# Moving twelve low-part subtractions from VectorE to GpSimd and all raw dot products into the first counting window, in a GAT + RGCN kernel

## The chip, the cores and the metric

One core of a Trainium2 chip runs the program. The metric is the device time of one execution in microseconds; the profile's span leaves out a small part at its ends. All times here are in microseconds (us) unless marked ns.

## The reference

A two-layer graph network on 625 nodes with 1024 features and 20000 edges (sorted by destination):

```python
h = x @ W
al, ar = h @ a_l, h @ a_r
e = exp(-leaky_relu(al[src] + ar[dst], 0.1))
rowsum = segment_sum(e, src)
h_prime = segment_sum(e[:, None] * h[dst], src) / (rowsum[:, None] + EPS)
x = layernorm(x + elu(h_prime))
# second layer: x @ root + bias + sum over 8 relations of mean-aggregated x @ weight[r], a gate, tanh, layernorm
```

## The kernel before, in words

**Precision.** Every fp32 matrix is split into a high part (a cast to fp32r) and a low part (`raw - high`, by a tensor_tensor subtraction); a product is three matmuls: high by high, low by high, high by low. So each operand costs one cast (ScalarE) and one subtraction (VectorE or GpSimd). The result is collected in PSUM.

**First product, h = xT by W.** W comes in two column halves of eight chunks (128x512) each, through a ring of four buffers (`w_raw`, `w_hi`, `w_lo`). SyncE loads a chunk when the low part four chunks earlier is made (line 337); ScalarE casts it when TensorE has used the buffer (line 527); VectorE makes `w_lo` (`split_low`, line 800). `w_lo_done` counts the low parts, for all chunks in order. h's first half (five tiles of 128 rows) is drained by ScalarE, a cast to `h_part(0, 0, t)` and a copy to `h_raw` (`copy_h`, line 551). `h_raw` shares memory with parts of the second half of h.

**Counting edges.** Edges are turned into a matrix of counts per destination, relation and source by one-hot matmuls, in 40 windows of 16 destinations. `oh_s` (one-hots of the sources, made in eight pieces at line 808 from two f16 tiles in SBUF) is the stationary side. For each pass over five edge tiles VectorE writes five `hot` buffers (line 931, a tensor_scalar of the f16 `table`, with a column of `key`), TensorE multiplies them (line 1281). A window has one pass or more. The five buffers are handed back and forth by the semaphores `built` and `counted`, so VectorE can be at most one pass ahead. ScalarE copies the window's counts out (line 568).

**What is woven into the windows.** After the passes of window w, each engine does other work, fixed by window numbers: TensorE the remaining items of W's second half in windows 0 to 6 (`items`, line 300; two or three items of three matmuls each), later the sums and transposes of counts and the attention's products (`att_h`, line 1253, from `hp_w(j)` on: windows 23, 25 and 33 for the first three tiles). VectorE: in window 0 the low parts of W's chunks 5 to 7 (`split_low(1, AHEAD + n)`), the five low parts of h's first half (`low_h`, line 875) and seven of ten dot products of h with a (`dot_raw`, line 888; `scalar_tensor_tensor` of `h_raw` and `a_bc`, both in SBUF, each waiting for the one before), the other three in windows 1 to 3; in windows 7 to 13 it drains h's second half; then, per destination tile j, `leaky`, `att_mult` (line 910; windows 20, 22, 30, 38 and after the last) and `att_low` (line 916; windows 22, 24, 32, 39 and after the last). ScalarE does `add_ar`, `exp_e` and `att_high` (the cast before `att_low`, in the window of `att_mult`). `tmp` has two buffers, so `add_ar(j)` waits for `att_low(j - 2)`.

**GpSimd** writes six iotas at the start and then waits until all 40 windows are counted (line 476); from then on it makes the low parts of all later weights (line 460). The last low parts of the kernel (line 465) run beside VectorE's `u - xf` (line 1104), two SBUF tiles of 128x1024.

The lines 1054, 1057 and 1059, named in the rows, belong to the second layer: a reduction of `C_hi`, a cast of `col_sum` (one SBUF tile of 128x640) and a subtraction of two SBUF tiles of 128x640.

Of the kernel before, what the change touches and what calls it, by code (L numbers as in the profile page):

```python
# [5 lines left out]
def gat_rgcn_kernel(nc, dst_cols, src_cols, type_cols, dst_units, xT, x, weights, a, bias, b_gate, counts_dram, out):  # L6
    f32 = mybir.dt.float32
# [5 lines left out]
    ALU = mybir.AluOpType  # L13
# [6 lines left out]
    KT = D // P  # L20
    NT = -(-N // P)
# [15 lines left out]
    WINDOWS = NP // WIN  # L37
# [14 lines left out]
    def rows(t):  # L52
        return P if t < NT - 1 else N - P * (NT - 1)
# [5 lines left out]
    with ctx:  # L59
# [6 lines left out]
        M_hi = [sb("M_hi0", [P, KT, NP], f32r)]  # L66
# [41 lines left out]
        def h_part(low, half, t, p=P):  # L108
            return h_parts[0:p, 2 * half + low, t, :]
# [58 lines left out]
        def bank(b, p=P, c0=0, c=H2):  # L168
            return ps[0:p, b * H2 + c0:b * H2 + c0 + c]
# [4 lines left out]
        def xw_bank(t):  # L174
            return t if t < NT - 1 else 7
# [118 lines left out]
        ALL = KT * NT  # L294
        AHEAD = 5
        SPREAD = 7
        DOTS_AHEAD = 7
        WARM = 8

        def items(w):  # L300
# [143 lines left out]
        @block.gpsimd  # L444
        def _(pool):
            pool.iota(iota_i[:, :], pattern=[[1, CODES], [P // 2, WIN]], base=0, channel_multiplier=0).then_inc(pool_consts, 1)
            pool.iota(part_col[:, :], pattern=[[0, 1]], base=0, channel_multiplier=1,
                      allow_small_or_imprecise_dtypes=True).then_inc(pool_consts, 1)
            pool.iota(iota_s[:, :], pattern=[[1, P]], base=0, channel_multiplier=0,
                      allow_small_or_imprecise_dtypes=True).then_inc(pool_consts, 1)  # L450
            pool.iota(iota_up[:, :, :], pattern=[[1, SUB], [SUB, UNITS]], base=1, channel_multiplier=0,
                      allow_small_or_imprecise_dtypes=True).then_inc(pool_consts, 1)
            pool.iota(iota_down[:, :, :], pattern=[[-1, SUB], [-SUB, UNITS]], base=1000, channel_multiplier=0,
                      allow_small_or_imprecise_dtypes=True).then_inc(pool_consts, 1)
            pool.iota(iota_body[:, :], pattern=[[BODY, ALL_TILES // BODY]], base=0, channel_multiplier=0,
                      allow_small_or_imprecise_dtypes=True).then_inc(pool_consts, 1)

            def split_chunk(n, k):
                pool.wait_ge(w_hi_done, 8 * n + k + 1)
                pool.tensor_tensor(w_lo[k % RING][:, :], w_raw[k % RING][:, :], w_hi[k % RING][:, :].bitcast(f32),  # L460
                                   ALU.subtract).then_inc(w_lo_done, 1)

            def last_chunk(k):
                pool.wait_ge(last_hi_done, k + 1)
                pool.tensor_tensor(last_w(1, k), last_raw[k][:, :], last_w(0, k).bitcast(f32),
                                   ALU.subtract).then_inc(last_lo_done, 1)

            def split_ahead(n, last=False):
                for k in range(KT):
                    if k < KT - RING:  # L470
                        split_chunk(n, k + RING)
                    elif not last:
                        split_chunk(n + 1, k + RING - KT)


            pool.wait_ge(window_counted, WINDOWS)
            for k in range(RING):
                split_chunk(SEG_Z, k)

            def x1_low(t):  # L480
                pool.wait_ge(x1_hi_done, t + 1)
                pool.tensor_tensor(x1_lo[0:rows(t), t, :], u[0:rows(t), t, :], x1_hi[0:rows(t), t, :].bitcast(f32),
                                   ALU.subtract).then_inc(x1_lo_done, 1)

            split_chunk(SEG_Z, RING)
            split_chunk(SEG_Z, RING + 1)
            x1_low(0)
            split_chunk(SEG_Z, RING + 2)
            x1_low(1)
            split_chunk(SEG_Z, RING + 3)  # L490
            x1_low(2)
            split_chunk(SEG_Z + 1, 0)
            x1_low(3)
            split_chunk(SEG_Z + 1, 1)
            x1_low(4)
            split_chunk(SEG_Z + 1, 2)
            split_chunk(SEG_Z + 1, 3)
            split_ahead(SEG_Z + 1)
            with pool.Fori(0, R // 2) as j:
                for half in range(4):  # L500
                    split_ahead(4 * j + SEG_U + half)
            split_ahead(SEG_U + 2 * R)
            pool.wait_ge(g_drained, ITEMS + ITEMS * R)
            for k in range(KT):
                split_chunk(SEG_U + 2 * R + 1 + (k + RING) // KT, (k + RING) % KT)
                if k < NT:
                    r = slice(0, rows(k))
                    pool.tensor_tensor(xf[r, k, :], x1_hi[r, k, :].bitcast(f32), x1_lo[r, k, :].bitcast(f32), ALU.add)\
                        .then_inc(xf_done, 1)
            split_chunk(SEG_G, RING)  # L510
            for k in range(3):
                last_chunk(k)
            split_chunk(SEG_G, RING + 1)
            for k in range(3, 5):
                last_chunk(k)
            split_chunk(SEG_G, RING + 2)
            for k in range(5, 7):
                last_chunk(k)
            split_chunk(SEG_G, RING + 3)
            last_chunk(7)  # L520
# [3 lines left out]
        def _(act):  # L524
# [25 lines left out]

            def copy_h(half, t):
                act.wait_ge(u_ready, NT * half + t + 1)
                nc.scalar.copy(h_part(0, half, t, rows(t)), bank(xw_bank(t), rows(t))).then_inc(h_hi_done, 1)
                if half == 0:
                    nc.scalar.copy(h_raw[0:rows(t), t, :], bank(xw_bank(t), rows(t))).then_inc(u_drained, 1)
# [216 lines left out]
        def _(dve):  # L772
# [27 lines left out]
            def split_low(n, k):  # L800
                dve.wait_ge(w_hi_done, 8 * n + k + 1)
                v.tensor_tensor(w_lo[k % RING][:, :], w_raw[k % RING][:, :], w_hi[k % RING][:, :].bitcast(f32),
                                ALU.subtract).then_inc(w_lo_done, 1)
# [68 lines left out]
            v.tensor_copy(lohi_row[:, :], ps[0:1, 6 * H2:6 * H2 + WINDOWS]).then_inc(row_done, 1)  # L872
            dve.wait_ge(row_done, 1)

            def low_h(t):
                r = slice(0, rows(t))
                dve.wait_ge(h_hi_done, t + 1)
                dve.wait_ge(u_drained, NT + t + 1)
                v.tensor_tensor(h_part(1, 0, t, rows(t)), h_raw[r, t, :], h_part(0, 0, t, rows(t)).bitcast(f32),
                                ALU.subtract).then_inc(h_lo_done, 1)  # L880

            def dot(half, lr, t, source, junk):
                r = slice(0, rows(t))
                at = (2 * half + lr) * NT + t
# [51 lines left out]
            for w in range(WINDOWS):  # L936
                first_pass = window_range(DVE_ENGINE, w)
                dve.reg_mod(tile_at, first_pass, STARTS)
                with dve.Fori(first_pass, LOOP_END, STARTS + BODY):
                    hots(w)  # L940
                if w == 0:
                    split_low(1, AHEAD)
                    for t in range(NT):
                        low_h(t)
                    split_low(1, AHEAD + 1)
                    dve.wait_ge(a_here, 16)
                    for n in range(DOTS_AHEAD):
                        dot_raw(n)
                    split_low(1, AHEAD + 2)
                elif w <= 2 * NT - DOTS_AHEAD:  # L950
                    dot_raw(DOTS_AHEAD + w - 1)
                if SPREAD <= w < AL_W:
                    a, b = [len(DRAINS) * n // (AL_W - SPREAD) for n in (w - SPREAD, w - SPREAD + 1)]
                    for t, piece in DRAINS[a:b]:
                        drain_h(t, piece)
                if w == AL_W:
                    dve.wait_ge(dot_done, 4 * NT)
                    step(v.tensor_tensor(alr[:, :], dots[:, 0:2 * NT], dots[:, 2 * NT:4 * NT], ALU.add))
                    for t in range(NT):
                        d = v.tensor_scalar(diag[:, t * P:(t + 1) * P], ident, alr[:, t:t + 1], None, ALU.mult)  # L960
                    d.then_inc(diag_done, 1)
                for j in range(NT):
                    if w == E_W[j] + 2:
                        leaky(j)
                for j in range(NT - 1):
                    if w == MULT_W[j]:
                        att_mult(j)
                for j in range(NT - 1):
                    if w == min(MULT_W[j] + 2, WINDOWS - 1):
                        att_low(j)  # L970

            att_mult(NT - 1)
            att_low(NT - 1)
            dve.wait_ge(sums_ready, 1)
            v.tensor_scalar(rowsum[:, :], bank(SUM_BANK, c=2 * NT).rearrange("p (t c) -> p t c", c=2)[:, :, 0],
# [554 lines left out]
```

## Time and profile before

| | us |
|---|---|
| median of 3 runs | 1001.15 |
| lowest, highest | 1000.7, 1001.23 |
| the profiled execution, device time | 1000.9 |
| its span | 998.8 |
| TensorE busy (share of the span) | 981.4 (98%) |
| VectorE busy | 391.7 (39%) |
| ScalarE busy | 281.1 (28%) |
| GpSimd busy | 255.0 (26%) |

The granted TensorE clock is full in all 40 slices of the span. Matmuls are pipelined and their recorded durations overlap, so their starts are to be read, not their lengths. In a timeline row the first number is the start from the span's start, the second the time until the last of the grouped instructions ended, x5 the number of them, and in brackets the idle time of the engine before it and what ended it. In the rows PE is TensorE, DVE VectorE, ACT ScalarE, POOL GpSimd.

### The profile page before, as it was taken

Reading aid. Unit: us, or ns where it says so; the run is one execution under the profiler, and the core shown is the slowest. Engines: PE = TensorE matmul, PEld = TensorE weight load, DVE = VectorE, ACT = ScalarE, POOL = GpSimd, SP = SyncE. Lnnn points to the kernel's source line nnn. Section 1 sums busy time; section 2 is a strip of 40 time slices with the busy share of each in tenths; the row PEclk is TensorE's granted clock in tenths of the full one; section 3 lists DMA queues with packets and bytes.
Section 4 is the critical chain, followed back from the end, with each engine's and each line's share of the span. In section 5 each row is a group of like instructions: output and inputs, shape, how many; then the busy total and the mean of one; then the engine's idle time right before and its main releaser. Section 6 shows DMA issues by size and latency. Waiting matters only on the chain.

```text
span 998.8 us, 14624 instructions
## 1 busy us (share of the span) xinstructions
PE 981.4 (98%) x5159; PEld 823.9 (82%) x5159; DVE 391.7 (39%) x746; ACT 281.1 (28%) x487; POOL 255.0 (26%) x196
## 2 busy tenths in 40 slices
PE   9997999999999999999999999999999999999997
PEld 7875677788888888888888888888888888888886
DVE  7979773721431430530430341232232233202277
ACT  4324542851122221221222222222212212212332
POOL 0000002055423223123122142142232232326730
PEclk9999999999999999999999999999999999999999
DMA  7303558066211411311321231141041041212402
GB/s 264 95 12 106 163 154 252 1 214 189 92 36 43 142 52 42 134 57 42 114 78 42 98 94 42 47 134 42 14 168 42 21 161 41 74 46 72 137 1 103
DMA packets 69005, 91.41 MB, mean 92 GB/s; under 512 B 9396, under 2 KB 35475, under 8 KB 68838
## 3 DMA queue, kind: packets, MB, share of 16 engines
q1 hardware_dynamic: 68966, 90.90, 29.0%
q8 instruction: 23, 0.38, 0.2%
q14 instruction: 16, 0.13, 0.0%
HBM read 75.19 MB, written 15.69 MB: 91 GB/s over the span
## 4 chain that ended last, share of the span: by engine, by line
PE 98%; DVE 1%; issue 1%; ACT 0%; POOL 0%; DVEq 0%; ACTq 0%
PE ps L1175 21%; PE ps L1177 21%; PE ps L1176 21%; PE ps L1431 9%; PE ps L1430 9%; PE ps L1281 6%; PE ps L1243 1%; PE ps L1256 1%; PE ps L1257 1%; PE ps L1258 1%; PE ps L1486 1%; PE ps L1485 1%; PE ps L1484 1%; PE ps L1264 1%; PE ps L1328 0%
## 5 line engine op out<-in xcount | busy, mean ns | idle before, releaser
L460 POOL TENSOR_TENSOR w_lo<-w_raw,w_hi 128x512 fp32r<-128x512 f32 x168 | 218.1, 1303 | 701.8 <-ACT w_hi L535 545.7
L535 ACT CAST w_hi<-w_raw 128x512 fp32r<-128x512 f32 x184 | 114.7, 623 | 466.0 <-PE ps L1177 396.0
L1175 PE MATMUL ps<-w_hi,M_hi 128*128 128x512 f32 (+1 forms) x550 | 215.6, 392 | 0.1
L1177 PE MATMUL ps<-w_lo,M_hi 128*128 128x512 f32 (+1 forms) x550 | 214.3, 390 | 0.0
L1176 PE MATMUL ps<-w_hi,M_lo 128*128 128x512 f32 (+1 forms) x550 | 214.2, 389 | 0.0
L1049 DVE SCALAR_TENSOR_TENSOR u<-ps,scale,u 128x512 f32<-128x512 f32 (+1 forms) x90 | 66.4, 744 | 314.2 <-PE ps L1177 314.2
L1430 PE MATMUL ps<-C_hi,x_hi 128*128 128x320 f32 (+3 forms) x640 | 184.4, 306 | 0.0
L1431 PE MATMUL ps<-C_hi,x_lo 128*128 128x320 f32 (+3 forms) x640 | 184.3, 306 | 0.0
L1175 PE MATMUL ps<-w_hi,M 128*128 128x512 f32 (+1 forms) x360 | 140.3, 390 | 0.0
L1177 PE MATMUL ps<-w_lo,M 128*128 128x512 f32 (+1 forms) x360 | 140.2, 390 | 0.0
L1176 PE MATMUL ps<-w_hi,M 128*128 128x512 f32 (+1 forms) x360 | 140.2, 389 | 0.0
L1430 PEld LDWEIGHTS ps<-C_hi,x_hi 128*128 128x128 f32 (+1 forms) x640 | 120.7, 189 | 0.9
L1175 PEld LDWEIGHTS ps<-w_hi,M_hi 128*128 128x128 f32 (+1 forms) x550 | 101.9, 185 | 23.5 <-issue 0.6
L1431 PEld LDWEIGHTS ps<-C_hi,x_lo 128*128 128x128 f32 (+1 forms) x640 | 120.9, 189 | 0.3
L1177 PEld LDWEIGHTS ps<-w_lo,M_hi 128*128 128x128 f32 (+1 forms) x550 | 101.8, 185 | 23.0
L1176 PEld LDWEIGHTS ps<-w_hi,M_lo 128*128 128x128 f32 (+1 forms) x550 | 101.9, 185 | 22.3
L1177 PEld LDWEIGHTS ps<-w_lo,M 128*128 128x128 f32 (+1 forms) x360 | 66.7, 185 | 15.0
L1176 PEld LDWEIGHTS ps<-w_hi,M 128*128 128x128 f32 (+1 forms) x360 | 66.7, 185 | 14.8
L1175 PEld LDWEIGHTS ps<-w_hi,M 128*128 128x128 f32 (+1 forms) x360 | 66.7, 185 | 14.5
L931 DVE TENSOR_SCALAR hot<-table,key 128x640 bf16<-128x640 f16 x210 | 65.7, 381 | 21.3 <-PE ps L1281 19.1
L1281 PE MATMUL ps<-hot,oh_s 128*128 128x320 bf16 x420 | 64.0, 299 | 3.2 <-DVE hot L931 1.3
L1054 DVE TENSOR_REDUCE col_sum<-C_hi 128x640 f32<-128x3200 f32 x8 | 47.9, 5992 | 43.5 <-DMA C_hi<-C_dram 43.5
(178 smaller groups left out, 771.9 us busy)
## 6 DMA issues: line engine op xcount, KB each, us to landing
w_raw<-weights SPq DMA_DIRECT2D x184, 256.0 KB, 2.8
C_dram<-Cst SPq DMA_DIRECT2D x25, 512.0 KB, 6.0
C_hi<-C_dram SPq DMA_DIRECT2D x8, 1600.0 KB, 7.0
z<-b_gate SPq DMA_DIRECT2D x5, 512.0 KB, 9.9
u<-bias SPq DMA_DIRECT2D x5, 512.0 KB, 7.6
xT_raw<-xT SPq DMA_DIRECT2D x8, 312.5 KB, 6.0
u<-x SPq DMA_DIRECT2D x4, 512.0 KB, 5.2
last_raw<-weights SPq DMA_DIRECT2D x8, 256.0 KB, 6.0
```

The source lines that it names most:

```text
L460: pool.tensor_tensor(w_lo[k % RING][:, :], w_raw[k % RING][:, :], w_hi[k % RING][:, :].bitcast(f32), ALU.subtract).then_inc(w_lo_done, 1)
L535: nc.scalar.copy(w_hi[k % RING][:, :], w_raw[k % RING][:, :]).then_inc(w_hi_done, 1)
L931: v.tensor_scalar(hot[:, s * NP:(s + 1) * NP], table[:, :], float(WIN * w), key[:, ds(tile + s, 1)], ALU.add, ALU.is_equal).then_inc(built ...
L1049: v.scalar_tensor_tensor(u[r, t, half * H2:(half + 1) * H2], bank(t, rows(t)), scale[odd][r, t:t + 1], u[r, t, half * H2:(half + 1) * H2], ...
L1054: v.tensor_reduce(col_sum[:, :], C_hi[:, :, :].bitcast(f32).rearrange("p m n -> p n m"), X, ALU.add)\
L1175: mm(o, lhs_hi[:, k, c], w_hi[k % RING][:, :], start=opens, stop=False)
L1176: mm(o, lhs_lo[:, k, c], w_hi[k % RING][:, :], start=False, stop=False)
L1177: last = mm(o, lhs_hi[:, k, c], w_lo[k % RING][:, :], start=False, stop=closes_)
L1243: last = mm(o, ident_r[:, :], Cst[j % 2][:, m0:m1, r, :], start=r == 0, stop=r == R - 1)
L1281: last = mm(bank(window_bank(w) + c, c=SPLIT), oh_s[:, ds(edge + s * P, P)], hot[:, s * NP + c * SPLIT:s * NP + (c + 1) * SPLIT], start=Fa ...
L1430: mm(o, x1_hi[r, m, f], C_hi[r, m, c0:c0 + cn], start=m == 0, stop=False)
L1431: last = mm(o, x1_lo[r, m, f], C_hi[r, m, c0:c0 + cn], start=False, stop=m == NT - 1)
```

## The change

GpSimd's program gets a part ahead of its wait for the last window: the five low parts of h's first half, then (when VectorE has made the first five low parts of W's second half, so that the count stays in order) those of chunks 5 to 7, then `att_low` for tiles 0 to 3. VectorE loses these and does all ten `dot_raw` in window 0, after the hots. ScalarE's copy of h's second half now waits for all five low parts of h; VectorE waits for the four low parts of the attention before its own last one, to keep the count in order. The hunks of the diff are, from the top, in GpSimd's, ScalarE's and VectorE's program; VectorE's own definition of `low_h` goes too.

```diff
+            def low_h(t):
+                pool.wait_ge(h_hi_done, t + 1)
+                pool.wait_ge(u_drained, NT + t + 1)
+                pool.tensor_tensor(h_part(1, 0, t, rows(t)), h_raw[0:rows(t), t, :], h_part(0, 0, t, rows(t)).bitcast(f32),
+                                   ALU.subtract).then_inc(h_lo_done, 1)
+
+            def att_low(j):
+                pool.wait_ge(attT_hi_done, j + 1)
+                pool.tensor_tensor(M_lo[0][:, j, :], tmp[j % 2][:, :], M_hi[0][:, j, :].bitcast(f32), ALU.subtract)\
+                    .then_inc(attT_lo_done, 1)
+
+            for t in range(NT):
+                low_h(t)
+            pool.wait_ge(w_lo_done, KT + AHEAD)
+            for k in range(AHEAD, KT):
+                split_chunk(1, k)
+            for j in range(NT - 1):
+                att_low(j)
 
             pool.wait_ge(window_counted, WINDOWS)
...
             def copy_h(half, t):
                 act.wait_ge(u_ready, NT * half + t + 1)
+                if half == 1:
+                    act.wait_ge(h_lo_done, NT)
...
                 if w == 0:
-                    split_low(1, AHEAD)
-                    for t in range(NT):
-                        low_h(t)
-                    split_low(1, AHEAD + 1)
                     dve.wait_ge(a_here, 16)
-                    for n in range(DOTS_AHEAD):
+                    for n in range(2 * NT):
                         dot_raw(n)
-                    split_low(1, AHEAD + 2)
-                elif w <= 2 * NT - DOTS_AHEAD:
-                    dot_raw(DOTS_AHEAD + w - 1)
...
-                for j in range(NT - 1):
-                    if w == min(MULT_W[j] + 2, WINDOWS - 1):
-                        att_low(j)
 
             att_mult(NT - 1)
+            dve.wait_ge(attT_lo_done, NT - 1)
             att_low(NT - 1)
```

## Rows read from the trace of the kernel before

**Rows 1.** The page, chain that ended last: share of the span by engine
```profile
PE 98%; DVE 1%; issue 1%; ACT 0%; POOL 0%; DVEq 0%; ACTq 0%
```

**Rows 2.** Waits, 60 to 180: us in total, times, longest
```profile
POOL w_lo L460 <- PE ps L1299: 155.8, 1, 155.8
...
PE ps L1296 <- ACT Cst L568: 4.2, 6, 0.8
...
PE ps L1281 <- DVE hot L931: 1.3, 3, 0.6
```

**Rows 3.** Timeline of VectorE, 30 to 42.5
```profile
37.19 0.69 DVE L802 TENSOR_TENSOR w_lo<-w_raw,w_hi 128x512 fp32r<-128x512 f32 x1 [0.82 <-ACT w_hi L535]
...
41.10 1.57 DVE L931 TENSOR_SCALAR hot<-table,key 128x640 bf16<-128x640 f16 x5 [1.12 <-issue]
```

**Rows 4.** Timeline of VectorE, 42 to 62 (first and last of seven dot products, then hots)
```profile
46.80 0.68 DVE L885 SCALAR_TENSOR_TENSOR M<-h_raw,a_bc 128x512 fp32r<-128x512 f32 x1
...
51.19 0.69 DVE L885 SCALAR_TENSOR_TENSOR M<-h_raw,a_bc 128x512 fp32r<-128x512 f32 x1
...
52.41 1.56 DVE L931 TENSOR_SCALAR hot<-table,key 128x640 bf16<-128x640 f16 x5
```

**Rows 5.** Timeline of TensorE, 48 to 59: counts of windows 0 and 1
```profile
51.27 1.52 PE L1281 MATMUL ps<-hot,oh_s 128*128 128x320 bf16 x10
...
54.19 2.88 PE L1281 MATMUL ps<-hot,oh_s 128*128 128x320 bf16 x20
```

**Rows 6.** Timeline of ScalarE, 30 to 50
```profile
35.95 0.70 ACT L555 COPY h_raw<-ps 113x512 f32<-113x512 f32 x1
...
44.66 0.62 ACT L535 CAST w_hi<-w_raw 128x512 fp32r<-128x512 f32 x1 [2.78 <-PE ps L1177]
48.06 0.62 ACT L535 CAST w_hi<-w_raw 128x512 fp32r<-128x512 f32 x1 [2.78 <-PE ps L1177]
```

**Rows 7.** VectorE's line 1104 (min/median/max ns), then the timelines, 954 to 957
```profile
L1104 DVE TENSOR_TENSOR u<-u,xf x5: 1225/1226/2198, 951.1 to 958.1; 128x1024 f32<-128x1024 f32 x4, 113x1024 f32<-113x1024 f32 x1
...
954.73 2.29 POOL L460 TENSOR_TENSOR w_lo<-w_raw,w_hi 128x512 fp32r<-128x512 f32 x1
...
955.91 2.20 DVE L1104 TENSOR_TENSOR u<-u,xf 128x1024 f32<-128x1024 f32 x1
```

**Rows 8.** Timelines of VectorE and of GpSimd, 253 to 263
```profile
254.43 5.94 DVE L1054 TENSOR_REDUCE col_sum<-C_hi 128x640 f32<-128x3200 f32 x1
260.40 0.49 DVE L1057 CAST col_parts<-col_sum 128x640 fp32r<-128x640 f32 x1
260.93 0.83 DVE L1059 TENSOR_TENSOR col_parts<-col_sum,col_parts 128x640 fp32r<-128x640 f32 x1
...
257.92 1.29 POOL L460 TENSOR_TENSOR w_lo<-w_raw,w_hi 128x512 fp32r<-128x512 f32 x1 [2.05 <-ACT w_hi L535]
261.32 1.59 POOL L460 TENSOR_TENSOR w_lo<-w_raw,w_hi 128x512 fp32r<-128x512 f32 x1 [2.11 <-ACT w_hi L535]
```

**Rows 9.** Timelines of VectorE, ScalarE and TensorE, 111.5 to 121 (windows 21 to 24)
```profile
111.57 3.04 DVE L931 TENSOR_SCALAR hot<-table,key 128x640 bf16<-128x640 f16 x10
114.53 0.82 DVE L913 SCALAR_TENSOR_TENSOR tmp<-tmp,att 128x640 f32<-128x640 f32 x1
...
116.00 3.04 DVE L931 TENSOR_SCALAR hot<-table,key 128x640 bf16<-128x640 f16 x10
...
113.05 0.71 ACT L600 CAST M_hi<-tmp 128x640 fp32r<-128x640 f32 x1
...
116.51 1.63 PE L1281 MATMUL ps<-hot,oh_s 128*128 128x320 bf16 x10 [0.45 <-DVE hot L931]
```

**Rows 10.** Timelines of VectorE, ScalarE and TensorE, 136 to 143 (windows 31 and 32)
```profile
136.82 3.07 DVE L931 TENSOR_SCALAR hot<-table,key 128x640 bf16<-128x640 f16 x10
...
137.93 0.73 ACT L600 CAST M_hi<-tmp 128x640 fp32r<-128x640 f32 x1
...
139.71 1.53 PE L1281 MATMUL ps<-hot,oh_s 128*128 128x320 bf16 x10 [0.15 <-issue]
```

More of the change, by code:

```diff
@@ L296, in gat_rgcn_kernel @@
         SPREAD = 7
-        DOTS_AHEAD = 7
         WARM = 8
@@ L873, in _ @@
             dve.wait_ge(row_done, 1)
[L875 to L880, printed above, removed]
             def dot(half, lr, t, source, junk):
```

## The prediction

> **What bounds the kernel now.** I read the chain of waits first: TensorE carries 98% of it and VectorE 1% [rows 1]. So only what moves a TensorE start can move the end, and the question for every part of the change is which waits of TensorE it removes or makes. The list of waits for the stretch in which the edge counting runs is next. TensorE waits for VectorE's edge hots (line 931) three times, 1.3 us in all, and for ScalarE's copies of the window counts 4.2 us; GpSimd does nothing for 155.8 us, until the last window is counted [rows 2]. That is the room in which the change puts 12 GpSimd instructions, and 1.3 us is about all that a freed VectorE can give back directly.
>
> Then the timelines around the first two windows. VectorE writes the hots of window 0 from 41.10 to 42.6, TensorE starts on them only at 51.27 [rows 3, 5]: it is busy with W's chunks until then. The hots of window 1 start at 52.41, behind VectorE's eight low parts and seven dot products, and TensorE starts them at 54.19 [rows 4, 5]. Where TensorE does wait for hots, it starts 0.51 after VectorE does (116.00 to 116.51) [rows 9]. So the hots of window 1 may start as late as 54.19 - 0.51 = 53.68 without cost: a slack of 1.27 us now.
>
> **The change, step by step.** Three low parts of W, five of h and four of the attention leave VectorE's queue for GpSimd's, 12 instructions; three dot products move from windows 1 to 3 into window 0.
>
> 1. VectorE in window 0. After the hots (41.10 + 5 x 0.30 = 42.6) only ten dot products remain. Seven of them start from 46.80 to 51.19 [rows 4], so one takes (51.19 - 46.80) / 6 = 0.73 and ten take 7.3: the hots of window 1 could start at 49.9 instead of 52.41, if nothing disturbs VectorE. Slack would grow to 53.7 - 49.9 = 3.8. TensorE gains nothing here, as it waits for nothing on VectorE at this place.
>
> 2. What GpSimd's work does to VectorE. The trace of before has one place where both run operations that read two SBUF tiles. There a VectorE subtraction that takes 1.226 alone takes 2.20, and the GpSimd instruction beside it takes 2.29 instead of 1.29 [rows 7, 8]. They take turns: the one that comes second stands still. One GpSimd instruction of 128x512 costs VectorE 2.20 - 1.23 = **0.97** per meeting. A second place agrees: GpSimd's subtraction at 261.32, issued while VectorE subtracts two SBUF tiles, takes 1.59 instead of 1.29; under VectorE's reduction of one SBUF tile (254.43 to 260.4) it keeps its 1.29 [rows 8]. So what matters is which kind VectorE runs. The one-hots (line 808) and low parts of W have two SBUF inputs, and so have the dot products (h_raw and a_bc). For the hots (one tile, f16) no row shows a meeting: bounds 0 and 0.97. Five hots take 1.57 and ten 3.04 [rows 3, 9], so 0.29 each for 640 elements, and the cast of 640 f32 elements takes 0.49 where the subtraction of 640 takes 0.83 [rows 8]. Both one-tile operations read faster than one input of the subtraction does, so I take them as using both inputs, and price a meeting at 0.97.
> The Trainium skill, "SBUF — State Buffer", section "Who interferes with whom", says the same of both kinds (two SBUF inputs; the two-port modes of tensor_scalar, copy and cast) and that the loser blocks for the whole instruction. The trace agrees on the blocking of the first kind; on its length it shows 0.97, not the full 1.29.
>
> 3. Count of meetings before window 1. GpSimd starts its five low parts of h as ScalarE's copies arrive, the last at 36.65 [rows 6], while VectorE is in an unbroken row of one-hots and low parts up to 39.9. Five meetings, 4.85, less the 0.82 that VectorE sat waiting for ScalarE before 37.19 [rows 3]: 4.03. Hots of window 0 then start at 45.1. Of W's three low parts, chunk 5's falls in the gap before these hots (1.12 of issue, [rows 3]) and costs nothing; chunk 6's (ScalarE's high part done at 45.28) meets the hots, chunk 7's (48.68) the dot products [rows 6]: 1.94 more. If GpSimd found no way in between VectorE's instructions, the meetings would only move into the dot products, each of which waits for the one before it; the sum is the same. VectorE reaches window 1 at 49.9 + 4.0 + 1.9 = 55.9 (rounded up), and TensorE waits 55.9 - 53.7 = **+2.2**.
> Cover: TensorE starts W's chunk 3 at 44.6 and chunk 4 at 48.0 (ScalarE's high parts of chunks 6 and 7 are released there, [rows 6]); VectorE's low parts of these two chunks slip from 37.9 and 39.9 to about 40.9 and 43.8. No cost; without this cover it would be up to 4. Chunks 5 to 7 are due from 52.7 on, GpSimd has them by 50. SyncE's loads, which wait for the low parts, slip by the same 3 to 4 and still land before ScalarE's copies. Windows 2 to 6 lose three dot products, but VectorE waits for TensorE there: nothing.
>
> 4. Attention, tile 0. ScalarE's high part ends at 113.76 [rows 9]; GpSimd's 128x640 subtraction starts there, 0.97 x 640 / 512 = 1.2 of blocking. VectorE is in the ten hots from 111.57 and then the multiply at 114.53 [rows 9]. It loses 1.2 and is spared att_low (0.74): hots of window 23 at 116.5 instead of 116.0, **+0.5** on TensorE. Without blocking it would be the 0.45 of wait gained [rows 9].
>
> 5. Tile 1: a meeting two windows later, in the ten hots from 116.00 [rows 9]; but there TensorE has the attention products of tile 0 to do between its counts, some 1.4 us of work, and VectorE is spared 0.74 behind them. Nothing. Tile 2: high part done at 138.66 [rows 10], VectorE in its hots 1.0 ahead of TensorE (window 32: 136.82 + 5 x 0.30 = 138.3, TensorE at 139.71, less 0.51). 1.2 of blocking leaves **+0.3**.
>
> 6. Tile 3 and the rest. Both engines are free at the end of the windows; GpSimd's first low parts of the next weights come some 1.1 later (they began at the end of the 155.8 [rows 2]), and their first reader comes only behind the attention's products. The new waits (ScalarE's copies of h's second half on all five low parts; VectorE's last att_low on four) are for things that are done by then: the low parts of h by 42, the copies come from window 6 on. 0.
>
> Sum: 2.2 + 0.5 + 0.3 = +3.0 on the profiled execution's 1000.9 (span 998.8 and 2.1 around it, which the change does not touch), 1003.9. The median of the runs shown is 0.25 higher, 1001.15, so **1004.1** against it. TensorE works through the stretch behind without idling, so nothing takes a delay back.
>
> **Rivals.** (A) No blocking matters here: GpSimd's work runs under VectorE's as if alone. VectorE reaches window 1 at 49.9, tile 0 gains 0.45, and the time is 1000.7: not slower. It decides if the meetings before window 1 cost VectorE under 3.8 together instead of 6. For it: no row shows a one-hot or a dot product slowed. Against it: [rows 7, 8]. (B) Only operations with two SBUF tiles meet; the hots do not. Then chunk 6 is free (2.2 - 1.0 = +1.2), tile 0 meets only the multiply, half way through (-0.2), tile 2 costs 0: +1.0, 1002.1, still no measurable change. For it: the reduction of one tile in [rows 8]; against it, the speed of the hots. (C) The loser stands for the whole 1.29 (1.6 for 640 columns). Seven meetings: 9.0 - 0.8 - 3.8 = 4.4, tile 0 0.9, tile 2 0.7: +6.0, 1007.1. That is the length by the page's rule; the rows give it less, as instructions overlap at their ends. (D) Faster by over 2: no mechanism; even all of 1.3 is below it.
>
> **How the numbers follow.** About 0.2% (2.0 us) can be told from no change. Forecast (all meet, 0.97) 0.60, A 0.17, B 0.14, C 0.07, D 0.02. The forecast's own spread is 1002.9 to 1005.4, from half a meeting more or less in each part, and a small part of it lies under 1003.15. Slower 0.60 + 0.07, less 0.05: 0.62. The range reaches from A's 1000.7 to 1005.8.
>
> **What would show it.** One-hots of line 808 stretched from 1.47 to about 2.45 between 33 and 44, dot products of 0.69 with a few near 1.6, hots of window 0 at about 45 and of window 1 near 55.9; a TensorE wait for hots of some 2 us from 54.2 on; GpSimd's low parts at up to 2.3. Wrong if VectorE's durations are unchanged (A), if only hots are (B), or if TensorE idles at some other place.

## The result and the profile after

The changed kernel takes 1006.46 us (median of 5 runs, 1005.58 to 1007.82) against 1000.92 of the kernel before: a ratio of 1.0059, 95% interval 1.0048 to 1.0071. It is slower, as forecast, but by 5.5 us instead of 3.0, and outside the range. The profiled execution is the slowest of the five in device time (1007.82), but not in its span: 1004.8, where the five spans run from 1003.6 to 1005.6. Against the span of before (998.8) it is 6.0 longer, and this is the difference that the traces have to explain. In device time the two profiled executions are 6.9 apart: 3.0 lies outside the span here and 2.1 did before.

In the chain of waits TensorE now carries 92% and VectorE 4%, where it was 98% and 1% [rows 1]:

```profile
PE 92%; DVE 4%; ACT 2%; issue 1%; DVEq 0%; POOL 0%; ACTq 0%
```

These shares say where the chain runs and not what was lost: 6% of the span is far more than 6.0 us. Up to window 1, for instance, the chain now goes through VectorE's row of work (one-hots from 38.4, hots, dot products), because TensorE waits for it at 57.17.

The waits of TensorE up to 340 us (total, number, longest; line numbers have moved: the counts are line 1284 now, the hots 943, the window copy 587). Its waits for hots were 1.3 in three, up to 340 us as in [rows 2]; its waits for ScalarE's copies are the same 4.2:

```profile
PE ps L1284 <- DVE hot L943: 5.1, 5, 2.7
PE ps L1299 <- ACT Cst L587: 4.2, 6, 0.8
```

VectorE from 30 to 62, the same stretch as in [rows 3, 4]:

```profile
35.23 1.47 DVE L827 TENSOR_TENSOR oh_s<-iota_s,src_h 128x2560 bf16<-128x2560 f16 x1
37.28 1.12 DVE L821 TENSOR_TENSOR w_lo<-w_raw,w_hi 128x512 fp32r<-128x512 f32 x1 [0.57 <-ACT w_hi L552]
38.33 2.57 DVE L827 TENSOR_TENSOR oh_s<-iota_s,src_h 128x2560 bf16<-128x2560 f16 x1
40.82 1.78 DVE L821 TENSOR_TENSOR w_lo<-w_raw,w_hi 128x512 fp32r<-128x512 f32 x1
...
43.82 4.62 DVE L943 TENSOR_SCALAR hot<-table,key 128x640 bf16<-128x640 f16 x5 [1.12 <-issue]
48.36 0.68 DVE L897 SCALAR_TENSOR_TENSOR M<-h_raw,a_bc 128x512 fp32r<-128x512 f32 x1
...
49.08 1.65 DVE L897 SCALAR_TENSOR_TENSOR M<-h_raw,a_bc 128x512 fp32r<-128x512 f32 x1
...
56.64 3.69 DVE L943 TENSOR_SCALAR hot<-table,key 128x640 bf16<-128x640 f16 x10
```

And GpSimd beside it:

```profile
32.97 12.02 POOL L477 TENSOR_TENSOR M<-h_raw,M 128x512 fp32r<-128x512 f32 x5 [30.44 <-ACT h_raw L574]
44.94 2.72 POOL L459 TENSOR_TENSOR w_lo<-w_raw,w_hi 128x512 fp32r<-128x512 f32 x2
48.85 1.33 POOL L459 TENSOR_TENSOR w_lo<-w_raw,w_hi 128x512 fp32r<-128x512 f32 x1 [1.19 <-ACT w_hi L552]
```

GpSimd's five low parts of h one by one (min/median/max ns):

```profile
L477 POOL TENSOR_TENSOR M<-h_raw,M x5: 1277/1735/4886, 33.0 to 43.7; 128x512 fp32r<-128x512 f32 x4, 113x512 fp32r<-113x512 f32 x1
```

The turns are plain to see. While VectorE's instructions follow one another without a gap (the one-hots to 36.7, still 1.47 each), GpSimd's first low part of h gets no turn: it starts at 32.97, takes 4.89 and gets through only once VectorE stands waiting for ScalarE, before 37.28. From then on the two alternate: VectorE's low parts take 1.12 and 1.78 instead of 0.68, a one-hot 2.57 instead of 1.47, the five hots of window 0 4.62 instead of 1.57 (so the hots do meet GpSimd), one dot product 1.65 instead of 0.69. That is 6.6 us of stretching. The hots of window 1 start at 56.64 instead of 52.41.

TensorE over the same stretch, counts of windows 0 and 1 (as [rows 5]), and then stretches of 2 us. In such a row stand the stretch, its length, TensorE's busy time with the number of instructions, the granted clock (1.00 is full), the busy share of the DMA engines and GB/s:

```profile
51.36 1.52 PE L1284 MATMUL ps<-hot,oh_s 128*128 128x320 bf16 x10
...
57.17 4.56 PE L1284 MATMUL ps<-hot,oh_s 128*128 128x320 bf16 x20 [2.75 <-DVE hot L943]
```

```profile
54.00:56.00 2.00, 0.42 (x4) 1.00 0.00 0
56.00:58.00 2.00, 0.83 (x5) 0.86 0.00 0
58.00:60.00 2.00, 2.00 (x9) 0.50 0.00 0
60.00:62.00 2.00, 2.00 (x13) 0.79 0.00 0
62.00:64.00 2.00, 2.00 (x15) 1.00 0.00 0
```

TensorE waits 2.75. Then its granted clock falls to 0.50, the lower of its two levels (1.2 GHz), and the twenty matmuls of window 1 take 4.56 instead of 2.88. The 0.86 and 0.79 are means of stretches that hold both levels. The end of window 1 is 4.66 later than before, and it stays 4.6 to 4.7 later up to window 20 and 4.8 at windows 21 and 22. Nothing takes it back.

The rest is lost at the attention. GpSimd's low part of tile 0 and VectorE's multiply and hots of windows 23 and 24 (as [rows 9]), then TensorE at windows 23 and 32:

```profile
118.48 3.02 POOL L482 TENSOR_TENSOR M_lo<-tmp,M_hi 128x640 fp32r<-128x640 f32 x1 [68.30 <-ACT M_hi L619]
...
119.29 0.82 DVE L925 SCALAR_TENSOR_TENSOR tmp<-tmp,att 128x640 f32<-128x640 f32 x1
120.02 5.64 DVE L943 TENSOR_SCALAR hot<-table,key 128x640 bf16<-128x640 f16 x10
...
121.83 1.63 PE L1284 MATMUL ps<-hot,oh_s 128*128 128x320 bf16 x10 [0.96 <-DVE hot L943]
...
146.10 1.04 PE L1284 MATMUL ps<-hot,oh_s 128*128 128x320 bf16 x6 [0.30 <-DVE hot L943]
```

Ten hots take 5.64 instead of 3.04: two turns of about 1.3, for tiles 0 and 1. The end of window 23 is 5.32 later than before, that of window 33 6.09, and about that it remains. Of the last step, 0.5 falls within window 32: it starts 5.37 later than before, TensorE does four of its ten matmuls and then stands for hots (the last row), and it ends 5.90 later. Another 0.2 comes between its end and the start of window 33, without a wait for hots in the list.

### The profile page after: what moved, and what is told of

It reads as the page before. It is cut to its first block, busy times and chain, and to the rows that moved or that the text cites. A ratio compares the mean times of both kernels' runs of the same rounds, so it can differ in the third digit from the quotient of the medians.

```text
span 1004.8 us, 14631 instructions
## 1 busy us (share of the span) xinstructions
PE 983.8 (98%) x5159; PEld 825.0 (82%) x5159; DVE 395.1 (39%) x734; ACT 281.2 (28%) x487; POOL 278.0 (28%) x208
## 4 chain that ended last, share of the span: by engine, by line
PE 92%; DVE 4%; ACT 2%; issue 1%; DVEq 0%; POOL 0%; ACTq 0%
PE ps L1178 20%; PE ps L1179 20%; PE ps L1180 20%; PE ps L1434 9%; PE ps L1433 9%; PE ps L1284 6%; PE ps L1246 1%; PE ps L1488 1%; PE ps L1489 1%; PE ps L1487 1%; DVE hot L943 1%; DVE M L897 1%; PE ps L1259 1%; PE ps L1261 1%; PE ps L1267 1%
## 5 line engine op out<-in xcount | busy, mean ns | idle before, releaser
L459 POOL TENSOR_TENSOR w_lo<-w_raw,w_hi 128x512 fp32r<-128x512 f32 x171 | 221.2, 1298 | 547.2 <-ACT w_hi L552 546.9
L943 DVE TENSOR_SCALAR hot<-table,key 128x640 bf16<-128x640 f16 x210 | 72.7, 414 | 22.9 <-PE ps L1284 19.4
L1057 DVE TENSOR_REDUCE col_sum<-C_hi 128x640 f32<-128x3200 f32 x8 | 47.9, 5990 | 42.5 <-DMA C_hi<-C_dram 42.5
```

What stands on the lines that cost most here:

```text
L943: v.tensor_scalar(hot[:, s * NP:(s + 1) * NP], table[:, :], float(WIN * w), key[:, ds(tile + s, 1)], ALU.add, ALU.is_equal).then_inc(built ...
L1057: v.tensor_reduce(col_sum[:, :], C_hi[:, :, :].bitcast(f32).rearrange("p m n -> p n m"), X, ALU.add)\
```

## Experiments

The theory: GpSimd's instructions and VectorE's take turns, so the moved work makes VectorE late instead of early; with the three dot products that come ahead on top, TensorE idles long enough to lose its clock as well. The rivals were these: the dot products alone, the turns alone, another cause for the slow window 1, or GpSimd's work really freeing VectorE. "Lag" below is how much later the end of a window is than before (the last matmul of its counts in the two traces), less the lag that the profile already has at window 0 (-0.4 to +0.7; it differs from profile to profile and was not traced). Beside these runs the kernel before took a median of 1000.85 to 1001.08, and the ratios are against that.

### e1: seven dot products in window 0, as before

```diff
-                    for n in range(2 * NT):
+                    for n in range(7):
                         dot_raw(n)
+                elif w <= 3:
+                    dot_raw(6 + w)
```

> The changed kernel, but only seven dot products in window 0 and one each in windows 1 to 3, as before. Theory (turns with GpSimd and the full row of dot products add up on VectorE): the hots of window 1 start 3 x 0.73 = 2.2 earlier than in the changed kernel, at 54.4 instead of 56.6, so TensorE waits 0.7 instead of 2.75 at window 1, and its granted clock does not fall behind it (1.7 saved); the attention part keeps its +1.5. Time about 1003. Rival (turns alone make it, the dot products are covered): still about 1006. Rival (the dot products alone make it): TensorE does not wait at window 1, 1002.4.

Measured: 1003.81 us (1002.96 to 1005.48), ratio 1.0026 [1.0016, 1.0036]. TensorE at window 1:

```profile
54.73 1.63 PE L1286 MATMUL ps<-hot,oh_s 128*128 128x320 bf16 x10 [0.64 <-DVE hot L943]
56.52 1.53 PE L1286 MATMUL ps<-hot,oh_s 128*128 128x320 bf16 x10 [0.16 <-issue]
```

The wait is 0.64 there, the granted clock 1.00 in every stretch from 50 to 68, the lag of window 1 1.2 instead of 4.6. So the turns do not make the loss at window 1 by themselves: 2.2 us of dot products are worth 3.4 in the traces, through the wait, the pace of the two passes (e2) and the clock. In the medians the two kernels are 2.7 apart; this profile is of one of the fastest runs of e1.

### e2: all dot products ahead, nothing on GpSimd

```diff
-                    for n in range(DOTS_AHEAD):
+                    for n in range(2 * NT):
                         dot_raw(n)
                     split_low(1, AHEAD + 2)
-                elif w <= 2 * NT - DOTS_AHEAD:
-                    dot_raw(DOTS_AHEAD + w - 1)
```

> The kernel before with all ten dot products in window 0 and nothing on GpSimd. Theory: VectorE reaches window 1 at 52.4 + 2.2 = 54.6, TensorE waits about 0.9 there, its clock stays full, no loss at the attention: 1001.8. Rival (the dot products alone make the loss at window 1): TensorE waits 2.7 and its clock falls, +4.6: 1005.5.

Measured: 1002.2 us (1001.67 to 1003.62), ratio 1.001 [1.0001, 1.0019]. TensorE at window 1:

```profile
55.65 1.63 PE L1279 MATMUL ps<-hot,oh_s 128*128 128x320 bf16 x10 [0.80 <-DVE hot L931]
57.44 1.53 PE L1279 MATMUL ps<-hot,oh_s 128*128 128x320 bf16 x10 [0.17 <-issue]
```

It waits 0.80, the clock stays at 1.00, the lag is 1.4. Neither cause makes the loss alone; both lie on the same engine and add up beyond its slack: 1.4 here and 1.2 in e1, but 4.6 together.

There is a term here that I had not priced. Counted from window 0 in each profile, TensorE starts window 1 0.94 later than before, but ends it 1.4 later. Window 1 has two passes. When its first hots come late, VectorE writes all ten in a row in 3.04, and TensorE, which follows them, needs 3.3 for both passes where it had 2.88. Counted from the end of the window, the slack was 0.45 shorter than the 1.27 that I read from its start.

### e5: VectorE late by its own work

```diff
                     for n in range(DOTS_AHEAD):
                         dot_raw(n)
+                    for n in range(6):
+                        step(v.scalar_tensor_tensor(h_part(1, 1, 2), h_raw[:, 0, :], 1.0, a_bc[:, 0:H2], ALU.mult, ALU.mult))
```

> The kernel before with six more products of 128x512 on VectorE in window 0 (results unused), nothing on GpSimd: VectorE is late by its own work. Theory (the length of TensorE's wait decides the granted clock, whatever caused it): hots of window 1 at 52.4 + 6 x 0.74 = 56.9, TensorE waits 3.1, and behind it the granted clock falls to 0.5 for some 3 us as in the changed kernel: +3.1 + 1.7 = 1005.7. Rival (the slow window 1 comes from GpSimd's work or from the pace of the hots): +3.1 alone, 1004.0.

Measured: 1006.78 us (1005.57 to 1007.12), ratio 1.0053 [1.0039, 1.0067]. TensorE at window 1, and the granted clock:

```profile
57.29 4.17 PE L1283 MATMUL ps<-hot,oh_s 128*128 128x320 bf16 x20 [3.08 <-DVE hot L931]
```

```profile
54.00:56.00 2.00, 0.21 (x3) 1.00 0.00 0
56.00:58.00 2.00, 0.71 (x3) 0.63 0.16 14
58.00:60.00 2.00, 2.00 (x9) 0.52 0.31 117
60.00:62.00 2.00, 2.00 (x15) 1.00 0.00 0
```

With GpSimd idle a wait of this length brings the same fall of the clock, so GpSimd's work is not what lowers it; that idle time is, e6 shows. The lag of window 1 is 4.5. The median is 1.1 above the 1005.7 that I expected; the profiled run is the fastest of the five.

### e6: TensorE kept at work where it waited

```diff
+                if w == 1:
+                    for _ in range(12):
+                        mm(bank(window_bank(w)).rearrange("p (a b) -> p a b", b=P), zeros[:, :],
+                           zeros[:, :].unsqueeze(1).broadcast_to([P, H2 // P, P]), start=False, stop=False, skip_group_check=True)
                 with pe.Fori(first_pass, LOOP_END, STARTS + BODY):
                     counts(w)
```

> The changed kernel with twelve matmuls of zeros (512 columns of bf16, added to the window's bank, 0.21 each, 2.6 in all) ahead of window 1's counts, where TensorE waited 2.75. Theory (the idle time lowers the clock): the granted clock stays full, window 1's twenty matmuls take 2.9 instead of 4.56, time 1.7 less than the changed kernel's, about 1004.8. Rival (the clock falls for another reason): as the changed kernel, about 1006.5.

Measured: 1005.07 us (1004.81 to 1006.26), ratio 1.0041 [1.0028, 1.0055]. TensorE at window 1, and the clock:

```profile
56.75 1.63 PE L1284 MATMUL ps<-hot,oh_s 128*128 128x320 bf16 x10
58.54 1.53 PE L1284 MATMUL ps<-hot,oh_s 128*128 128x320 bf16 x10 [0.16 <-issue]
```

```profile
56.00:58.00 2.00, 1.88 (x12) 1.00 0.00 0
58.00:60.00 2.00, 1.84 (x15) 1.00 0.00 0
```

The hots of window 1 are as late as in the changed kernel (56.22, which is 56.53 on the clock of the kernel before), but the clock stays at its upper level and the lag of window 1 is 3.3 instead of 4.6: the clock costs 1.25. (I expected 1.7, as I had counted the 0.44 of the two passes to it.) In the times the two kernels are 1.4 apart, with overlapping runs; the traces are the firmer evidence.

### e3 and e4: the attention's low parts alone

e3 is the changed kernel with the attention's low parts on VectorE again, e4 the kernel before with nothing but them on GpSimd. The diff of e3 against the changed kernel (e4 has the opposite edits, against the kernel before: GpSimd gets `att_low`, VectorE loses it and waits for the four before its own last one):

```diff
-            for j in range(NT - 1):
-                att_low(j)
...
+                for j in range(NT - 1):
+                    if w == min(MULT_W[j] + 2, WINDOWS - 1):
+                        att_low(j)
```

> The changed kernel with the attention's low parts on VectorE as before (the low parts of W and h and the ten dot products as in the change). Theory: the loss at window 1 stays (+4.6), the loss at windows 22, 23 and 32 (+1.5) goes: 1005.0. Rival (the attention part is neutral, all is lost at window 1): as the changed kernel, 1006.5.

> The kernel before with only the attention's low parts of tiles 0 to 3 on GpSimd. Theory: +0.7 at windows 21 to 23 and +0.7 at 32 and 33, no change at window 1: 1002.3. Rival (no turns with the hots, the multiply is freed): -0.45, 1000.5.

Measured: e3 1005.26 us (1005.22 to 1006.96), ratio 1.005 [1.0036, 1.0064]; e4 1002.4 us (1001.42 to 1004.02), ratio 1.0013 [1.0004, 1.0022]. In e4's trace the lag at window 1 is 0, grows to 0.4 at window 23 and 1.1 at window 33; in e3's it is 4.3 at window 1, takes 0.5 more at window 21, and does not grow at windows 22 to 33. What makes the 0.5 at window 21, where the changed kernel loses 0.1, was not traced. VectorE and GpSimd in e4:

```profile
115.73 5.64 DVE L939 TENSOR_SCALAR hot<-table,key 128x640 bf16<-128x640 f16 x10
```

```profile
114.46 2.75 POOL L478 TENSOR_TENSOR M_lo<-tmp,M_hi 128x640 fp32r<-128x640 f32 x1 [111.93 <-ACT M_hi L608]
```

Against the kernel before, e4's rival (0.45 gained) falls: moving four subtractions of 0.74 off VectorE makes the kernel slower. Against the changed kernel, e3's median is 1.2 lower, but the runs overlap, so it is e4 and the lags on which this reading rests.

### e7: GpSimd writes only

The kernel leaves out the five low parts of h; GpSimd writes the same tiles with memsets instead.

```diff
-                pool.tensor_tensor(h_part(1, 0, t, rows(t)), h_raw[0:rows(t), t, :], h_part(0, 0, t, rows(t)).bitcast(f32),
-                                   ALU.subtract).then_inc(h_lo_done, 1)
+                pool.memset(h_part(1, 0, t, rows(t)).bitcast(f32), 0.0).then_inc(h_lo_done, 1)
```

> The changed kernel with GpSimd's five low parts of h replaced by memsets of the same tiles (they read nothing; the low part of h is left out). Theory (what meets are GpSimd's reads of SBUF with the second input of VectorE's operations): the one-hots, low parts and dot products of VectorE keep their 1.48, 0.68 and 0.69 beside them; W's low parts of chunks 5 to 7 still meet hots and one dot product. VectorE reaches window 1 at 49.9 + 2 to 3 = 52 to 53, TensorE does not wait at window 1: +1.5 from the attention, 1002.4. Rival (any GpSimd instruction takes turns): window 1 late as in the changed kernel if a memset is as long, +1 to +6.

Measured: 1002.69 us (1002.17 to 1003.91), ratio 1.0019 [1.001, 1.0029]. VectorE and GpSimd:

```profile
34.66 1.48 DVE L826 TENSOR_TENSOR oh_s<-iota_s,src_h 128x2560 bf16<-128x2560 f16 x1
...
41.04 2.60 DVE L942 TENSOR_SCALAR hot<-table,key 128x640 bf16<-128x640 f16 x5 [1.11 <-issue]
...
52.82 1.57 DVE L942 TENSOR_SCALAR hot<-table,key 128x640 bf16<-128x640 f16 x5
```

```profile
34.75 0.53 POOL L477 MEMSET M<- 128x512 f32 x1 [0.45 <-ACT h_raw L573]
```

Beside the memset both keep their time (1.48 and 0.53); beside W's low parts the hots and two dot products are still stretched by about 1.0 each. So a GpSimd instruction that only writes SBUF takes no turns with operations that have two SBUF inputs, and one that also reads does. The Trainium skill, "SBUF — State Buffer", section "Who interferes with whom", says that a VectorE instruction with two SBUF inputs contends with a GpSimd instruction that reads SBUF and not with one that only writes it; this run agrees. No memset ran beside hots. The hots of window 1 start at 52.82, three meetings behind 49.9, and window 1 has no lag.

### e8 and e9: what one moved instruction is worth

e8 is the changed kernel with h's five low parts on VectorE again, ahead of the dot products; e9 the kernel before with only W's three low parts on GpSimd. First e8 against the changed kernel (VectorE's definition of `low_h` comes back too), then e9 against the kernel before:

```diff
-            for t in range(NT):
-                low_h(t)
             pool.wait_ge(w_lo_done, KT + AHEAD)
...
                 if w == 0:
+                    for t in range(NT):
+                        low_h(t)
                     dve.wait_ge(a_here, 16)
```

```diff
+            pool.wait_ge(w_lo_done, KT + AHEAD)
+            for k in range(AHEAD, KT):
+                split_chunk(1, k)
...
-                    split_low(1, AHEAD)
...
-                    split_low(1, AHEAD + 1)
...
-                    split_low(1, AHEAD + 2)
```

> The changed kernel with h's five low parts back on VectorE (in window 0, ahead of the dot products). Theory (an instruction given to GpSimd saves VectorE 0.61 and costs it about 1.0): VectorE does 3.1 more but loses five meetings, less the 0.6 it used to lose waiting for ScalarE; hots of window 1 at 49.9 + 3.1 + 3 meetings = 55.9 to 56, hardly earlier than 56.6. TensorE waits about 2.1, clock uncertain: 1004.3 to 1006. Rival (giving work to GpSimd frees VectorE): 3.1 later than the changed kernel, 1009.6.

> The kernel before with only W's low parts of chunks 5 to 7 on GpSimd. Theory (each saves VectorE 0.61 and costs it about 1.0 in a turn): the hots of window 1 start 1.0 to 1.2 later than before, at 53.4 to 53.6, within the slack that ends at 53.7, so the time does not change: 1000.9. Rival (they free VectorE): hots of window 1 at 50.6, time unchanged too; the start of the hots tells them apart.

Measured: e8 1005.73 us (1005.45 to 1007.89), ratio 1.0058 [1.0044, 1.0071]; e9 1001.61 us (1000.55 to 1002.21), ratio 1.0005 [0.9996, 1.0014]. VectorE in the kernel before (a subtraction takes 0.61 from its start to the next one's), then in e8, then in e9:

```profile
42.58 0.68 DVE L802 TENSOR_TENSOR w_lo<-w_raw,w_hi 128x512 fp32r<-128x512 f32 x1
43.19 3.09 DVE L879 TENSOR_TENSOR M<-h_raw,M 128x512 fp32r<-128x512 f32 x5
```

```profile
40.68 2.61 DVE L948 TENSOR_SCALAR hot<-table,key 128x640 bf16<-128x640 f16 x5 [1.11 <-issue]
43.21 4.19 DVE L896 TENSOR_TENSOR M<-h_raw,M 128x512 fp32r<-128x512 f32 x5
...
48.77 1.65 DVE L902 SCALAR_TENSOR_TENSOR M<-h_raw,a_bc 128x512 fp32r<-128x512 f32 x1
```

```profile
43.90 4.19 DVE L883 TENSOR_TENSOR M<-h_raw,M 128x512 fp32r<-128x512 f32 x5
...
54.10 3.05 DVE L935 TENSOR_SCALAR hot<-table,key 128x640 bf16<-128x640 f16 x10
```

With five instructions more on VectorE, e8 reaches window 1 at 55.60, or 56.0 on the clock of the kernel before (its profile is 0.42 ahead at window 0); the changed kernel does at 56.55. So giving the five to GpSimd made VectorE 0.5 later, and the rival, by which e8 would be 3.1 later than the changed kernel, falls. In e9 three turns cost 1.0 (hots), 1.1 (the five low parts of h, 4.19 instead of 3.09) and 1.0, 3.1 together, against the 1.83 saved (3 x 0.61); the hots of window 1 start at 53.8 on the clock of before, 1.4 later. I expected at most 53.6 and no wait. Window 1 lags 0.7, which fits a slack that ends at 53.2 and not at 53.7 (e2), but the time cannot be told from that of before.

### e10: the same work where VectorE idles

h's five low parts go to GpSimd one by one behind the counts of windows 1 to 5, all dot products into window 0; W's and the attention's stay on VectorE. GpSimd's part of the diff (ScalarE's copies wait as in the change, and VectorE loses `low_h` and has all ten `dot_raw` in window 0):

```diff
+            for t in range(NT):
+                pool.wait_ge(window_counted, 2 + t)
+                pool.wait_ge(u_drained, NT + t + 1)
+                pool.tensor_tensor(h_part(1, 0, t, rows(t)), h_raw[0:rows(t), t, :], h_part(0, 0, t, rows(t)).bitcast(f32),
+                                   ALU.subtract).then_inc(h_lo_done, 1)
```

> The kernel before with h's five low parts on GpSimd, one behind each of windows 1 to 5's counts, where VectorE idles over 1 us per window, and all ten dot products in window 0; W's and the attention's low parts stay on VectorE. Theory (a turn costs only where VectorE has no idle time before TensorE needs its hots): hots of window 1 at 52.4 - 3.05 + 2.2 = 51.6, hots of windows 3 to 6 stretched by about 1 each but no wait of TensorE: 1000.9. Rival (any turn with the hots delays TensorE): +1 for each of four or five windows, 1005.

Measured: 1001.87 us (1000.9 to 1003.31), ratio 1.0007 [0.9998, 1.0016]: no change that can be told. VectorE:

```profile
45.98 0.69 DVE L810 TENSOR_TENSOR w_lo<-w_raw,w_hi 128x512 fp32r<-128x512 f32 x1 [2.05 <-ACT w_hi L541]
...
54.41 3.04 DVE L939 TENSOR_SCALAR hot<-table,key 128x640 bf16<-128x640 f16 x10
57.61 5.24 DVE L939 TENSOR_SCALAR hot<-table,key 128x640 bf16<-128x640 f16 x10 [0.16 <-issue]
63.14 2.61 DVE L939 TENSOR_SCALAR hot<-table,key 128x640 bf16<-128x640 f16 x5 [0.29 <-PE ps L1285]
```

My 51.6 for window 1 was wrong: without h's low parts ahead of it, the low part of W's chunk 6 comes up 2.05 too early and waits for ScalarE, and the dot products wait behind it. But the question is answered. The hots of windows 2 to 6 are stretched by 1.0 each (2.61 for five), and TensorE's lag is the same, 0.5, from window 1 to window 7. The rival (+1 for each) falls.

## Why the prediction was wrong

The direction held, and so did the mechanism as far as it went: GpSimd's instructions take turns with VectorE's. The size failed, in **step 3**, which put the loss at window 1 at +2.2 and left out what TensorE's clock does behind such a wait. The loss measured 4.6:

- Hots of window 1: put at 55.9, measured 56.55 (56.64 less the 0.09 of window 0), 0.65 more. Seven of the eight instructions cost time, as I had counted, but others than I thought: the first low part of h ran mostly while VectorE waited for ScalarE, one ran in the gap ahead of the hots, and six met in full, three of them the hots of window 0 (I had put one there, and chunk 5's low part into the gap). The six cost 6.2, 1.03 each where I put 0.97: 0.96 for a dot product, 1.0 to 1.1 for hots, one-hots and low parts. The first cost 0.4, so the wait for ScalarE took up some 0.5 and not the 0.82 that I took off. Together that is 6.6 instead of 6.0.
- The slack: it was put to end at 53.7, from the start of window 1; counted from the window's end, with its two passes, it ended at 53.2 (e2). That is 0.45 more.
- The clock: not in the sum at all, and without a reason given. After 2.75 of waiting TensorE ran at its lower level, 1.25 more (e6), and e5 shows that a wait brings it without any work on GpSimd. I took the waiting time for the whole cost of a wait. This is the largest of the three.

2.2 put, 0.65, 0.45 and 1.25 give the 4.6 measured.

Steps 1 and 2 held: no gain on TensorE at window 0, turns of about 1.0, and the hots do take part. That had been concluded from their speed alone, and the trace of the changed kernel shows it against rivals A and B. **Step 4** (+0.5): TensorE's wait for the hots of window 23 is 0.96 instead of 0.45; held. **Step 5**: nothing at tile 1, held; tile 2 cost 0.7 instead of 0.3, of which 0.5 is the wait within window 32. What made the other 0.2, ahead of window 33, stays open, and so does the 0.1 at window 21 that is counted to step 4 here. **Step 6**: no cost seen.

The sum of 3.0 thus became 4.6 + 0.65 + 0.7 = 5.95 in a span that is 6.0 longer. Rival C, +6.0, came out near this total by luck: its turns were to last 1.29, or 1.6 for 640 columns, and they lasted about 1.0 and 1.3.

The changed kernel's five runs spread over 2.2 us, where the five of before lay within 0.5. That is no mark of the change: in the longer series beside the experiments the kernel before spread over 1.8 to 2.3.

## What to carry to other kernels

Before moving work from VectorE to GpSimd, look at what VectorE does meanwhile: where it runs operations with two SBUF inputs, or one-input operations like the hots here, a moved subtraction of 512 f32 columns cost VectorE about 1.0 us in these traces, more than the 0.61 that it saved there. It did no harm that could be measured where VectorE waits anyway (e10). Measure slack from the end of a dependent group, not its start. Where the change makes a new wait of TensorE as long as those here (2.2 to 3.1 us), price the slow matmuls behind it too.

## What the runs showed of the hardware

- TensorE idle for 0.64 and 0.80 ahead of window 1 (e1, e2): granted clock 1.00 in every stretch. Idle for 2.2 (e8), 2.5 (e3), 2.75 (changed kernel) and 3.1 (e5): stretches at 0.50 to 0.52 behind it. With twelve matmuls of zeros in the gap (e6): 1.00.
- GpSimd's first low part of h in the changed kernel got no turn beside VectorE's unbroken row of one-hots and low parts: it took 4.9, until VectorE waited for another engine. Its later ones got their turns between VectorE instructions that also followed one another without a gap (one-hot 2.57, low part 1.78, hots 4.62 for five). What decides this is not shown. Beside dot products, each of which waits for the one before it, it got a turn soon: 1.33 for GpSimd, 1.65 for the dot product (both at 49).
- A GpSimd memset (0.53 for 128x512) and VectorE's two-input operations did not disturb one another (e7).
